# Expert rows of batches 1 to 3 summed by TensorE over diagonals of the scores

## The reference, cut to what matters

```python
logits = x @ router_weight.T + router_bias
top_val, top_idx = jax.lax.top_k(logits, TOP_K)
top_val = jax.nn.softmax(top_val, axis=-1)
...
out = jnp.einsum('etd,edh->eth', (up + 1.0) * glu, down_proj) + down_proj_bias[:, None, :]
out = out * router_scores.T[:, :, None]
out = out.sum(axis=0)
```

## Time and profile before

| | us |
|---|---|
| median of 3 runs | 1001.44 |
| lowest and highest run | 998.96, 1005.4 |
| profiled execution: its own time | 1002.28 |
| profiled execution: span | 1000.5 |

### The profile page before, as it was taken

How to read it: one execution, slowest core, us unless ns; L and a number is a source line. 1 busy time by engine, 2 the same in 40 slices (tenths; PEclk the granted TensorE clock), 3 DMA queues, 4 the chain that set the end, 5 groups by cost and what they waited for, 6 DMA issues and landing times. The chain is left out here.

```text
span 1000.5 us, 17431 instructions
## 1 busy us (share of the span) xinstructions
PE 918.0 (92%) x5629; PEld 734.0 (73%) x5629; DVE 757.0 (76%) x2032; ACT 589.6 (59%) x1711; POOL 506.6 (51%) x418
## 2 busy tenths in 40 slices
PE   7999999999389988995889999999999999999978
PEld 6355656566267755663678889988999889999966
DVE  6754755333885788999798888798897898888785
ACT  1752444446524678774666667747767567756743
POOL 3265667652533322434475656565654755646650
PEclk9988999999699999998999999999999999999999
DMA  9625222214101010000020000201001010000201
GB/s 325 275 66 229 77 72 85 78 75 166 63 1 61 6 80 2 2 22 1 22 64 1 22 23 1 64 2 36 8 2 64 1 44 1 1 23 1 97 1 43
DMA packets 19657, 55.18 MB, mean 55 GB/s; under 512 B 3264, under 2 KB 9488, under 8 KB 19056
## 3 DMA queue, kind: packets, MB, share of 16 engines
q1 hardware_dynamic: 13968, 40.68, 11.4%
q0 software_dynamic: 4512, 12.33, 3.5%
q10 hardware_dynamic: 1088, 1.05, 0.3%
HBM read 45.78 MB, written 8.26 MB: 54 GB/s over the span
## 5 line engine op out<-in xcount | busy, mean ns | idle before, releaser
L2499 ACT ACTIVATE y<-bank,g_mx 128x256 f32<-128x256 f32 x256 | 117.5, 486 | 115.5 <-DVE g_mx L2682 115.5
L2783 POOL TENSOR_TENSOR y<-y,g_sm 128x1024 f32<-128x1024 f32 x64 | 120.0, 1895 | 25.4 <-DVE g_sm L2698 25.4
L2759 POOL TENSOR_TENSOR g_c<-arena 128x1024 fp32r<-128x1024 f32 x30 | 64.0, 2132 | 112.4 <-DVE arena L2603 112.4
L2372 PE MATMUL bank<-arena 128*128 128x256 f32 x512 | 116.3, 380 | 0.0
L2372 PEld LDWEIGHTS bank<-arena 128*128 128x128 f32 x512 | 94.9, 190 | 12.0 <-issue 0.2
L763 PE MATMUL bank<-arena 128*128 x188 | 89.9, 601 | 0.0
L2255 PE MATMUL bank<-cst,y 128*128 128x128 f32 x512 | 71.9, 274 | 11.0 <-POOL y L2783 6.3
L2682 DVE TENSOR_REDUCE g_mx<-bank 128x2 f32<-128x512 f32 x128 | 79.3, 677 | 0.2 <-PE bank L2372 0.2
L1091 DVE TENSOR_SCALAR arena<-bank 128x256 f32<-128x256 f32 x47 | 19.9, 424 | 76.1 <-PE bank L763 65.2
L2349 PE MATMUL bank<-g_qh,g_xs 128*128 128x256 f32 x256 | 66.7, 298 | 7.4 <-POOL g_xs L2733 7.3
L884 POOL DMA_INDIRECT b_pairs<-arena x47 | 47.3, 1006 | 45.6 <-ACT arena L858 35.8
(11 more groups left out here) (427 smaller groups left out, 2676.5 us busy)
## 6 DMA issues: line engine op xcount, KB each, us to landing
arena<-in_dram SPq DMA_DIRECT2D x16, 768.0 KB, 15.7
arena<-in_dram SPq DMA_DIRECT2D x21, 512.0 KB, 3.7
arena<-b_pairs SPq DMA_DIRECT2D x8, 512.0 KB, 7.4
arena<-in_dram SPq DMA_DIRECT2D x3, 1024.0 KB, 4.8
arena<-in_dram SPq DMA_DIRECT2D x2, 704.0 KB, 4.8
x<-in_dram SPq DMA_DIRECT2D x4, 256.0 KB, 5.3
cx<-in_dram SPq DMA_DIRECT2D x4, 256.0 KB, 5.4
cxT<-in_dram SPq DMA_DIRECT2D x4, 256.0 KB, 5.7
```

Of the source, the lines that this page charges most:

```text
L2372: m = pe.matmul(o[:, st * 256:st * 256 + 256], g_t[:, c, st * P:st * P + P], keys, start=True, stop=True)
L2499: m = act.activation(g_p[:, c, st, :], o[:, st * 256:st * 256 + 256], ACT.Exp, bias=g_mx[j % 2][:, 2 * c + st:2 * c + st + 1], accum_out=g ...
L2759: pool.tensor_tensor(cat, g_o[j % 2], g_om, ALU.subtract).then_inc(s_gc, 1)
L2783: pool.tensor_tensor(pf, pf, sums, ALU.mult).then_inc(s_gp, 1)
```

## The change

Batches 1 to 3 no longer pass through ACT's scaling and POOL's additions. ACT writes, for each pair slot of a row tile, a diagonal matrix with the scores (the identity times one score per partition, 128x128), 8 for a batch, into free space of the arena: those of batch 1 in stage B ahead of the key transposes, those of batches 2 and 3 at the start of its stage M. PE multiplies each diagonal with its block of `b_back` and sums the four in PSUM (`B_sum_pe`, 8 products of 128x256 a batch), all three batches right behind the key transposes and ahead of layer C. DVE adds the bank to `x` (`B_add_dve`). Besides, key product 11 moves between the two halves of the table, and one small operation of DVE (`b_sp`) moves ahead of `place_dve`.

```diff
+        for b in range(1, B):
+            plan(("B", "sum", b), 3 + b)
...
-            table(range(T))
-            for n in range(11, 14):
+            table(range(0, 4))
+            K_raw_pe(pe, 11)
+            table(range(4, T))
+            for n in range(12, 14):
                 K_raw_pe(pe, n)
...
+            B_diagonals_act(act, 1)
             for n in range(NK):
                 K_tr_act(act, n)
...
+        def B_diagonals_act(act, b):
+            act.wait_ge(s_cst, 16)
+            if b == 1:
+                act.wait_ge(s_bs, 2)
             for t in (2 * b, 2 * b + 1):
                 for k in range(TOPK):
-                    m = act.activation(b_back[:, TOPK * t + k, :], b_back[:, TOPK * t + k, :], ACT.Identity,
-                                       scale=b_sc[:, t, k:k + 1])
-            m.then_inc(s_bsc, 1)
...
+                    m = act.activation(diagonal(t, k), ident, ACT.Identity, scale=b_sc[:, t, k:k + 1])
+            m.then_inc(s_bdg, 1)
+
+        def B_sum_pe(pe, b):
+            o = claim(pe, ("B", "sum", b))
+            pe.wait_ge(s_bk[b], 32)
+            pe.wait_ge(s_bdg, b)
+            for q in range(2):
+                t = 2 * b + q
+                for k in range(TOPK):
+                    m = pe.matmul(o[:, q * D:q * D + D], diagonal(t, k), b_back[:, TOPK * t + k, :], start=(k == 0),
+                                  stop=(k == TOPK - 1))
+            fill(m, ("B", "sum", b))
+
+        def B_add_dve(dve, b):
+            o = take(dve, ("B", "sum", b))
+            xb = x[:, 2 * b:2 * b + 2, :].rearrange("p t d -> p (t d)")
+            empty(dve.tensor_tensor(xb, xb, o[:, :], ALU.add), ("B", "sum", b))
+            have(dve, ("B", "sum", b))
...
         def M_pe(pe):
+            for b in range(1, B):
+                B_sum_pe(pe, b)
...
         def M_act(act):
-            B_scale_act(act, 1)
+            for b in HIGH:
+                B_diagonals_act(act, b)
             D_down_act(act)
             for b in LOW:
-                B_scale_act(act, b + 2)
...
         def M_pool(pool, C):
-            ln_pool(pool, C, K_C, EPS, batches=(0,))
-            B_combine_pool(pool, C, 1)
-            ln_pool(pool, C, K_C, EPS, batches=(1,))
-            B_combine_pool(pool, C, 2)
-            ln_pool(pool, C, K_D, EPS, batches=(0,))
-            B_combine_pool(pool, C, 3)
-            ln_pool(pool, C, K_D, EPS, batches=(1,))
+            ln_pool(pool, C, K_C, EPS, batches=LOW)
+            ln_pool(pool, C, K_D, EPS, batches=LOW)
```

More of the change, by code:

```diff
@@ L900, in B_pool, with diagonal @@
                 store(j)
-        s_bsc, s_bcb = sem("b_pairs_scaled"), sem("b_combined")
-        def B_scale_act(act, b):
-            act.wait_ge(s_bk[b], 32)
+        s_bdg = sem("b_score_diagonals")
+        b_dg = arena[:, 13312:13312 + 6 * TOPK * P].rearrange("p (n q) -> p n q", q=P)
+        def diagonal(t, k):
+            return b_dg[:, TOPK * (t - 2) + k, :]
+        def B_diagonals_act(act, b):
+            act.wait_ge(s_cst, 16)
+            if b == 1:
+                act.wait_ge(s_bs, 2)
             for t in (2 * b, 2 * b + 1):
                 for k in range(TOPK):
-                    m = act.activation(b_back[:, TOPK * t + k, :], b_back[:, TOPK * t + k, :], ACT.Identity,
-                                       scale=b_sc[:, t, k:k + 1])
-            m.then_inc(s_bsc, 1)
[L912 to L923, removed]
+                    m = act.activation(diagonal(t, k), ident, ACT.Identity, scale=b_sc[:, t, k:k + 1])
[15 more added lines that the diff above has]
+            have(dve, ("B", "sum", b))
         def B_combine_dve(dve, V, b):
@@ L1009, in place_dve @@
             V.sync()
-            V.do(dve.tensor_scalar(b_sp, const("iota")[:, 0:NTP], float(P), const("spare"), ALU.mult, ALU.add))
             for t in range(T):
@@ L1071, in B_dve @@
             dve.wait_ge(s_bc, 16)
+            V.do(dve.tensor_scalar(b_sp, const("iota")[:, 0:NTP], float(P), const("spare"), ALU.mult, ALU.add))
             place_dve(dve, V)
@@ L3132, in M_dve @@
                 else:
-                    B_combined_dve(dve, b)
+                    B_add_dve(dve, b)
                 ln_open_batch(dve, V, b)
```

## The result

| | before | changed |
|---|---|---|
| median of 6 runs, us | 1001.33 | 992.31 |
| lowest and highest | 998.96, 1005.4 | 989.02, 994.29 |
| ratio, 95% interval | | 0.9908 (0.9885 to 0.993) |
| span of the profiled execution | 1000.5 | 991.0 |

The change gains 9.0 us on the medians, 7.0 to 11.5 by the interval, and 9.5 between the two profiled spans.

What follows compares the result with a forecast made beforehand. It took a PE hole at 250.4 to 262.5 us, with VectorE standing still beside GpSimd's additions, as the bound. -3.9 - 3.0 + 1.4 - 0.6 = -6.1 us on 1002.28 gave 996.2, 995.4 for the median; range 989 to 1000.5.

Steps and rivals of the forecast that it cites:

- Part 1: Diagonals ahead of the key chunks on ACT: eight cost 2.4 us, sixteen 4.8; PE follows, through at 250.9.
- Part 2: Sums on PE ahead of layer C: 0.43 us a product, three batches 10.3 us, first transposes at 263.0.
- Part 3: DVE up to layer C's first addition: 5.0 us of standstill lost, addition at 266.3, 3.9 us gained, PE's sums limiting.
- Part 4: From layer C's first addition to stage D's first gate product: second L293 pair undisturbed, 3.0 us more gained.
- Part 5: High half: DVE adds two banks behind its last split, ahead of the first hidden part; 1.4 us lost.
- Part 6: The table with key product 11 between its halves: 0.6 us gained, between nothing and 2.2; first gather 1.7 to 3.6 later.
- rival 2: Denser table removes or moves low clock at 57 to 62 and 79 to 86 us: up to 5.9 us more, 989.5; 13%.
- the zero for `b_sp`: Moving this small DVE operation ahead of the one-hots was counted as no gain, at most 1.3 us.
- the forecast's own range: The forecast case, without the rivals, was given 992 to 998.5 us and 62%.
- Rival 1: Sums run at half the clock: +7.7 us, 1009; half of it at the lower clock takes 3.4 off the gain; 8%.
- Rival 3: Gain given back behind 284 us, where another chain rules: most of 5.5 us goes, 999 to 1001; 15%.

Runs made afterwards that it cites:

- Experiment 4: The changed kernel with GpSimd again doing additions of the old shapes in their old queue places, into memory nobody reads: 999.99 us, ratio 0.998 to the kernel before.
- experiment 7: The changed kernel with VectorE adding the banks of batches 2 and 3 ahead of layer C's first addition: 991.06 us, ratio 0.9889 to the kernel before.
- experiment 1: The kernel before with only key product 11 moved between the table's halves: 996.6 us for 1000.91, ratio 0.9958.
- experiment 8: The changed kernel, batch 3's sum behind layer C's batch 0 product, no products on constants there, late additions in VectorE's wait for ScalarE: 988.36 us, ratio 0.9874.

## Why the prediction was right

**What bounds the kernel** was read rightly in the main: the hole at 250 to 262 us hung on VectorE, and VectorE on GpSimd's additions. Experiment 4 shows that cause by itself. The Trainium skill (SBUF — State Buffer, "Who interferes with whom") lets a VectorE instruction in a two-port mode, or one with two SBUF inputs, be blocked by GpSimd, and others not. The traces agree as far as they show it: beside GpSimd's additions the L293 with one input (261.97 to 264.41, with L915 until 264.26) and the multiplication with two were held up, while before the change the reduction L1172 (265.79) and the addition from PSUM L1194 (277.97) took their usual 0.69 and 0.68 us. Whether L293 ran in a two-port mode, no row shows.

Two readings were off, and neither moved the sum. More of the kernel before's rows:

```profile
255.65 1.37 DVE L1183 TENSOR_SCALAR arena<-arena 128x512 int32<-128x512 int32 x1
257.06 1.38 DVE L1185 TENSOR_SCALAR arena<-arena 128x512 f32<-128x512 f32 x1
258.00 3.30 ACT L908 ACTIVATE arena<-arena 128x256 f32<-128x256 f32 x8
259.19 0.69 DVE L1189 TENSOR_TENSOR arena<-arena 128x512 f32<-128x512 f32 x1
```

VectorE's rounding was through at 259.88, and ACT's scales, which released TensorE, started only at 261.20, when ACT was through with its own scalings L908. So TensorE waited last for those scalings, and not for the rounding; it cost nothing, since layer C's first addition came at 270.22, when VectorE was through with batch 1. And L1183 and L1185, 0.43 us each where nothing disturbs them, were held up too, as was L1174 (0.47 us at 266.51 for 0.17): VectorE stood still for 7.2 us ahead of that addition, not 5.0.

**Part 1**, diagonals: 2.4 and 4.8 us forecast, 2.44 and 4.77 measured. **Part 2**, the sums: 10.3 and 10.6, at the full clock; the first transposes came at 259.17, 17.9 us after the return of the rows, and 263.0 - 245.1 is 17.9. **Part 3**: the first addition 21.2 us after the return of the rows for 25.1, 3.9 less as forecast, with TensorE as its limit; VectorE waited for it 2.56 us and not 0.4, for the 2.2 us of standstill that I had not counted. **Part 4**: 10.6 us from there to D's first product for 13.6, 3.0 less as forecast. **Part 5**: 1.4 us forecast; TensorE's wait grew by 1.1 us, from 0.49 to 1.60, and 1.3 us are lost behind D's first product, of which experiment 7 leaves the clock's part open.

**Part 6 was mis-sized, and it is nearly the whole difference**: 0.6 us forecast, at most 2.2, and 3.8 measured (4.2 on the median of experiment 1). I had priced the key product under a clock that would fall all the same, and my upper bound counted the lower level from 57 us on only. In the kernel before it began earlier, inside the table (length; PE, PEld, DVE, ACT, POOL; granted clock third from the end):

```profile
55.00:55.50 0.50, 0.50 (x4) 0.42 (x3) 0.50 (x2) 0.00 (x0) 0.00 (x0) 0.69 0.00 0
55.50:56.00 0.50, 0.50 (x4) 0.50 (x3) 0.50 (x2) 0.00 (x0) 0.00 (x0) 0.50 0.00 0
```

From about 55.3 to 62.0 us at half the clock is some 3.4 us lost, an estimate that leaves 0.4 of the 3.8. With the clock full, the table and product 11 together take 6.0 us from start to start for 9.2 (51.38 to 57.35, and 51.30 to 60.48), and product 12 takes 1.8 for 2.5. That the clock might not fall I had as rival 2, at 13%, and did not tie it to this edit firmly enough; for the table it was not a rival but what the edit does. In the two profiles with the table in one piece the clock falls at it, in the eleven that have 512-wide or filler products in its middle it does not. The delay of the first gather, which I had put at 1.7 to 3.6 us, was 0.4 for the same reason. Nothing speaks against the zero for `b_sp`. That the median still lies inside the forecast's own range, by 0.3 us, is luck; the whole range was wide enough to hold most of rival 2, and half of rival 2 came true.

**Rival 1** didn't happen. The Trainium skill (TensorE: Matmul & The Clock Gate, "What's actually happening") has the throttled state as the default that activity releases. The sums agree with that so far as the clock was full when they began and stayed so (1.00 from 247.0 to 257.4 us); whether dense sums bring back a fallen clock, no run shows, since it had not fallen. The table fits it less: there the clock fell while TensorE was busy for 5.73 of 5.80 us. Rival 1's seed is there, though: TensorE's idle 2.6 us behind the loop, which the diagonals of batch 1 cause, stands in all ten profiles that have them, and in four of these a low stretch in the key chunks followed, at a cost below 1 us each. In its price for half the sums at the lower level I had a slip: half of the 13.8 us by which the first result would come later is 6.9 us, not 3.4. **Rival 3**, a gain given back late, didn't happen beyond part 5. **Rival 2's** second half, the low stretch in the loop's first rounds, stayed in the changed kernel.

## What to carry to other kernels

Before GpSimd is given elementwise work to relieve VectorE, look at the longest and the median duration of VectorE's instructions beside it: here they stood four to six times apart (2697 and 693 ns, 2439 and 410), and that was a stop. Moving the work to TensorE, even as full 128x128 diagonals at 0.43 us a product, was cheaper than those standstills. When a shortened chain hangs on a new queue, put only what the chain needs ahead of it; one batch's sum and four fillers fewer brought stage D 1.8 us nearer here. A run of narrow products is a place to look at the granted clock: here a wide product that was due anyway, put in its middle, won 3.8 us and delayed the first gather by 0.4.

## What was not expected of the hardware

- TensorE was busy for 5.73 of 5.80 us while the clock fell: 32 products with 48 moving columns, 0.18 us from start to start on the mean. Product 11 (1.4 us from start to start) or four products of 128x256 in the middle kept the level of 2.4 GHz.
- The low stretches move about. Where the one near 75 us was filled, or did not come, one appeared at about 235 us (three profiles, one of them without a filler); but experiment 4's kernel has one near 75 and one at 240 us, and the profile of experiment 8 a short one near 80 us alone. That filling one brings on another is thus not shown.
- GpSimd's operation on two columns (L331) took 1.36 us at 264.32 in the changed kernel, where its median is 0.22. VectorE's two subtractions for the down weights (L1281, 1.78 us) had started before it, at 264.15, and were through at 265.93, 0.25 us after it. So the stop goes both ways.
